# Attention with a causal bound at 64 tokens: 1280 instead of 1536 score columns per step

## The reference

```
qkv = x @ W_attn.T                       # 4 query sets, one set of keys, one of values
for g in range(4):
    att = einsum(q_g, k) / sqrt(8)       # 16 heads of 8 channels, 256 queries x 256 keys
    att = softmax(where(causal, att, -inf))
    out_g = einsum(att, v)
return concat(out_g) @ W_proj.T
```

## Time and profile before

| | us |
|---|---|
| median of 3 runs | 800.66 |
| lowest, highest | 800.66, 803.36 |
| the profiled execution | 800.58 |
| its span | 798.9 |

### The profile page before, as it was taken

How to read it: one execution, slowest core, us unless ns; L and a number is a source line. 1 busy time by engine, 2 the same in 40 slices (tenths; PEclk the granted TensorE clock), 3 DMA queues, 4 the chain that set the end, 5 groups by cost and what they waited for, 6 DMA issues and landing times.

```text
span 798.9 us, 20426 instructions
## 1 busy us (share of the span) xinstructions
PE 757.4 (95%) x7674; PEld 412.7 (52%) x7674; DVE 648.9 (81%) x1917; ACT 719.9 (90%) x932; POOL 560.2 (70%) x685
## 2 busy tenths in 40 slices
PE   5898999999999999999999999999999999999996
PEld 3345667777774333333333333333334777677774
DVE  7998999999876667777778787788566898989885
ACT  5918999999999999999999999999997999899984
POOL 2897676655437888888898888888896445444442
PEclk9999999999999999999999999999999999999999
DMA  9110000000133333442444334433500000000000
GB/s 279 61 70 29 1 2 2 2 2 1 23 94 99 98 90 89 90 99 78 96 108 106 90 88 92 90 78 96 106 2 2 1 15 16 15 14 16 15 15 18
DMA packets 37962, 45.70 MB, mean 57 GB/s; under 512 B 6137, under 2 KB 23810, under 8 KB 37858
## 3 DMA queue, kind: packets, MB, share of 16 engines
q1 hardware_dynamic: 37858, 44.33, 22.4%
HBM read 27.53 MB, written 16.78 MB: 55 GB/s over the span
## 4 chain that ended last, share of the span: by engine, by line
PE 56%; ACT 18%; DVE 12%; issue 10%; POOL 2%; DMA 0%; ACTq 0%; DVEq 0%; POOLq 0%
PE psum L1006 15%; PE psum L937 14%; ACT prob L1272 13%; PE psum L1316 12%; PE psum L1263 5%; PE psum L1374 4%; DVE mixed L1025 4%; PE psum L1154 2%; ACT hidden_first L951 2%; ACT hidden_parts_first L953 1%; PE psum L686 1%; DVE hidden_parts_first L960 1%; POOL yhat L666 1%; DVE prod L656 1%; DVE stats L362 1%
## 5 line engine op out<-in xcount | busy, mean ns | idle before, releaser
L1272 ACT ACTIVATE prob<-psum 128x1536 f32<-128x1536 f32 x256 | 347.6, 1503 | 14.5 <-PE psum L1263 14.5
L1279 POOL TENSOR_SCALAR_AFFINE_SELECT prob<-prob 128x512 f32<-128x512 f32 (+3 forms) x448 | 304.8, 709 | 42.2 <-ACT prob L1272 32.1
L1316 PE MATMUL psum<-prob,vstack 128*32 128x256 f32 (+1 forms) x2048 | 204.9, 495 | 1.6 <-DVE o_tok L1324 1.6
L937 PE MATMUL psum<-xt_parts,w_parts 128*128 128x512 f16 x768 | 186.6, 379 | 0.0
L1025 DVE SCALAR_TENSOR_TENSOR mixed<-psum,comb_y,mixed 128x128 f32<-128x128 f32 x512 | 143.1, 339 | 1.5 <-PE psum L1006 1.5
L967 POOL TENSOR_TENSOR hidden_parts_second<-hidden_second,hidden_parts_second 128x512 f16<-128x512 f32 x64 | 77.2, 1207 | 93.6 <-ACT hidden_parts_second L953 93.6
L967 POOL TENSOR_TENSOR hidden_parts_first<-hidden_first,hidden_parts_first 128x512 f16<-128x512 f32 x64 | 79.4, 1241 | 73.2 <-ACT hidden_parts_first L953 73.2
L1263 PE MATMUL psum<-qstack,kstack 32*128 32x512 f16 x768 | 99.8, 385 | 9.1 <-ACT prob L1272 7.7
L1263 PEld LDWEIGHTS psum<-qstack,kstack 32*128 32x128 f16 x768 | 24.9, 91 | 157.3 <-ACT prob L1272 138.7
L937 PEld LDWEIGHTS psum<-xt_parts,w_parts 128*128 128x128 f16 x768 | 71.0, 98 | 64.0 <-issue 1.4
L951 ACT ACTIVATE hidden_second<-psum,b 128x512 f32<-128x512 f32 x128 | 88.3, 690 | 15.6 <-PE psum L937 12.1
(11 more groups left out here) (148 smaller groups left out, 840.9 us busy)
## 6 DMA issues: line engine op xcount, KB each, us to landing
qstack<-qk_parts SPq DMA_DIRECT2D x128, 128.0 KB, 3.6
qk_parts<-parts SPq DMA_DIRECT2D x64, 192.0 KB, 3.1
kstack<-qk_parts SPq DMA_DIRECT2D x128, 32.0 KB, 3.5
stream<-u_folded SPq DMA_DIRECT2D x4, 512.0 KB, 8.0
kept_x<-stream SPq DMA_DIRECT2D x4, 512.0 KB, 2.7
out<-mixed SPq DMA_DIRECT2D x7, 256.0 KB, 2.3
w_whole<-L_ffn_W SPq DMA_DIRECT2D x1, 1024.0 KB, 8.9
taps<-c_taps SPq DMA_DIRECT2D x1, 640.0 KB, 7.1
```

What stands on the lines that cost most here:

```text
L937: last = e.matmul(bank(u % 4), m.w1[:, w_part, ex, cols], xt_parts[:, s, x_part, :], start=(n == 0), stop=(n == len(PRODUCTS) - 1))
L1272: e.activation(prob[:, n % PROBS, :], psum[:, TILE * (n % 2):TILE * (n % 2 + 1)], ACT.Exp, scale=SCALE)\
L1279: return e.affine_select(kept, kept, [[0, kept.shape[1]], [0, 2], [sign, P]], ALU.is_ge, 0.0, base=0, channel_multiplier=-sign)
L1316: last = e.matmul(to[SLOT * lane:SLOT * (lane + 1)], vstack[:, b % 2, keys, first:first + SLOT], weights_of(n - t, lane, keys, pair), star ...
```

## The change

- The causal bound is drawn at 64 tokens inside each half of 128. Of each half, its first 64 keys (`EARLY`) meet all its 128 queries, and its last 64 keys (`LATE`) only its last 64 queries. The first half's 128 keys meet the second half's queries unmasked (`ACROSS`). The two halves' EARLY scores share a bank (64 partitions each), the LATE ones half a bank. A lane then has 512 + 256 + 512 = 1280 columns, and so has a step.
- `tensor_scores`: steps 0 and 1 of a quad issue six matmuls (two halves each of two EARLY and one LATE), of 64 columns of the array each; steps 2 and 3 issue two ACROSS of 128 columns of the array and two LATE halves of 64.
- Masks: six selects a quad in place of seven: two tiles of 768 columns for the second half's rows and again for the first half's rows, and one place of 512 (the LATE blocks of two steps) twice. A place's second select waits for its first by a semaphore and comes in the queue behind the first select of the next place.
- Sums: three a quad (EARLY 512, ACROSS 512, LATE 256) in steps 1, 2 and 3. EARLY waits for the masks of both 768-column places, ACROSS for the quad's four exponentials, LATE for all masks. The slot's two places hold the halves; the values exist in three forms.
- `PROBS` is 8, and an exponential waits for all sums of the quad two back.
- Around it: three input transpositions instead of two, 15 value matmuls instead of 6, three value copies instead of one, three row transpositions instead of one, two more memsets in the first experts.

```diff
+EARLY, LATE, ACROSS = range(3)
+BLK = P // 2
+STEPS_Q = (((EARLY, 0, 0), (EARLY, 1, BANK), (LATE, 2, 2 * BANK)),
+           ((EARLY, 2, 0), (EARLY, 3, BANK), (LATE, 1, 2 * BANK)),
+           ((ACROSS, 0, 0), (ACROSS, 1, BANK), (LATE, 3, 2 * BANK)),
+           ((ACROSS, 2, 0), (ACROSS, 3, BANK), (LATE, 0, 2 * BANK)))
+COLS = 2 * BANK + SETS * BLK
+SUMS_Q = (EARLY, ACROSS, LATE)
+MASKS_Q = 3
+PROBS = 8
...
-        for h in range(HALVES):
-            last = e.transpose(bank(at_bank(b))[:, h * P:(h + 1) * P], normed[:, HALVES * b + h, :], eye[:])
+        for at, h in ((0, 1), (P, 1), (P + BLK, 0)):
+            last = e.transpose(bank(at_bank(b))[:, at:at + P], normed[:, HALVES * b + h, :], eye[:])
...
+        places = [(slice(0, P), P, ACROSS)]
+        places += [(slice(BLK * half, BLK * (half + 1)), P * half + BLK * kind, kind) for kind in (EARLY, LATE)
+                   for half in range(HALVES)]
+        for rows, first_token, kind in places:
             for i, (w_part, x_part) in enumerate(PRODUCTS):
-                last = e.matmul(bank(6)[:, h * P:(h + 1) * P], at_x[:, s, x_part, h * P:(h + 1) * P],
+                last = e.matmul(bank(6)[rows, kind * P:(kind + 1) * P],
+                                at_x[:, s, x_part, first_token:first_token + rows.stop - rows.start],
...
+        for kind, lane, col in STEPS_Q[t]:
             at = slice(SLOT * lane, SLOT * (lane + 1))
+            queries = qstack[at, s, c].rearrange("p g (h l q) -> p h l g q", h=HALVES, q=BLK)
+            if kind == ACROSS:
+                last = e.matmul(to[:, col:col + BANK], kstack[at, s, c, P:2 * P], queries[:, 0], start=True, stop=True)
+                continue
+            for half in range(HALVES):
+                rows = slice(BLK * half, BLK * (half + 1))
+                key = P * half + BLK * kind
+                if kind == EARLY:
+                    moving, place = queries[:, half], to[rows, col:col + BANK]
+                else:
+                    moving, place = queries[:, half, 1], to[rows, col:col + SETS * BLK]
+                last = e.matmul(place, kstack[at, s, c, key:key + BLK], moving, start=True, stop=True)
...
+    def gpsimd_second_half_mask(e, m):
+        q, t = divmod(m, MASKS_Q)
+        e.wait_ge(exped, 4 * q + t + 1 + t // 2)
+        gpsimd_masked(e, mask_place(m), 0).then_inc(half_masked, 1)
+    def gpsimd_first_half_mask(e, m):
+        e.wait_ge(half_masked, m + 1)
+        gpsimd_masked(e, mask_place(m), 1).then_inc(masked, 1)
     def gpsimd_mask(e, n):
+        q, t = divmod(n, 4)
+        if t != 2:
+            m = MASKS_Q * q + min(t, 2)
+            gpsimd_second_half_mask(e, m)
+            if m:
+                gpsimd_first_half_mask(e, m - 1)
...
+    def tensor_weigh(e, q, kind, last_of_quad):
+        b, c = divmod(q, QUADS)
+        if kind == EARLY:
...
+                e.wait_ge(turned, q)
+            e.wait_ge(masked, MASKS_Q * q + 2)
+        elif kind == ACROSS:
+            e.wait_ge(exped, 4 * (q + 1))
         else:
+            e.wait_ge(masked, MASKS_Q * (q + 1))
...
-            if n >= 4:
-                at = n - n % 4 - 4
-                for i in ((), (0,), (1, 2), (3,))[n % 4]:
-                    tensor_weigh(e, at + i)
+            if n >= 4 and n % 4:
+                kind = SUMS_Q[n % 4 - 1]
+                tensor_weigh(e, n // 4 - 1, kind, kind == SUMS_Q[-1])
```

More of the change, by code:

```diff
@@ L1215, in tensor_v, with v_moves @@
             e.wait_ge(attn_done, HALVES * (BATCH - 2))
-        for h in range(HALVES):
+        places = [(slice(0, P), P, ACROSS)]
+        places += [(slice(BLK * half, BLK * (half + 1)), P * half + BLK * kind, kind) for kind in (EARLY, LATE)
+                   for half in range(HALVES)]
+        for rows, first_token, kind in places:
             for i, (w_part, x_part) in enumerate(PRODUCTS):
-                last = e.matmul(bank(6)[:, h * P:(h + 1) * P], at_x[:, s, x_part, h * P:(h + 1) * P],
+                last = e.matmul(bank(6)[rows, kind * P:(kind + 1) * P],
+                                at_x[:, s, x_part, first_token:first_token + rows.stop - rows.start],
                                 wqkv_parts[:, w_part, SETS + 1, :], start=(i == 0), stop=(i == len(PRODUCTS) - 1))
         last.then_inc(v_up, 1)
[L1222 to L1226, removed]
+    def v_moves(b):
+        source = bank(6)[:, 0:3 * D].rearrange("p (k n d) -> p k n d", n=HEADS, d=HD)
+        places = vstack[:, b % 2, :, :, :, 0:HD]
+        for half in range(HALVES):
+            rows = slice(BLK * half, BLK * (half + 1))
+            yield places[rows, 0:2, :, half], source[rows, 0:2]
+        yield places[:, ACROSS, :, 0], source[:, ACROSS]
     def scalar_v_first(e):
         e.wait_ge(v_up, 1)
-        e.wait_ge(zeroed, 3)
-        e.mul(v_places(0), v_source(), 1.0 / WSCALE).then_inc(v_copied, 1)
+        e.wait_ge(zeroed, 4)
+        for place, source in v_moves(0):
+            last = e.mul(place, source, 1.0 / WSCALE)
+        last.then_inc(v_copied, 1)
     def vector_v(e, b):
@@ L1235, in vector_v @@
         if b >= 2:
-            e.wait_ge(weighed, STEPS_B * (b - 1))
-        e.tensor_scalar(v_places(b), v_source(), 1.0 / WSCALE, None, ALU.mult).then_inc(v_copied, 1)
+            e.wait_ge(weighed, SUMS_B * (b - 1))
+        for place, source in v_moves(b):
+            last = e.tensor_scalar(place, source, 1.0 / WSCALE, None, ALU.mult)
+        last.then_inc(v_copied, 1)
     def step_of(n):
@@ L1256, in tensor_scores @@
             e.wait_ge(s_stack[s], STACK * (b // 2 + 1))
-        for i, (lane, keys, pair) in enumerate(STEPS_Q[t]):
+        for kind, lane, col in STEPS_Q[t]:
             at = slice(SLOT * lane, SLOT * (lane + 1))
[L1259 to L1264, removed]
+            queries = qstack[at, s, c].rearrange("p g (h l q) -> p h l g q", h=HALVES, q=BLK)
+            if kind == ACROSS:
+                last = e.matmul(to[:, col:col + BANK], kstack[at, s, c, P:2 * P], queries[:, 0], start=True, stop=True)
+                continue
+            for half in range(HALVES):
+                rows = slice(BLK * half, BLK * (half + 1))
+                key = P * half + BLK * kind
[4 more added lines that the diff above has]
+                last = e.matmul(place, kstack[at, s, c, key:key + BLK], moving, start=True, stop=True)
         last.then_inc(scored, 1)
@@ L1295, in weights_of, with gpsimd_masked @@
[L1295 to L1313, removed]
+    def gpsimd_masked(e, kept, half):
+        sign = 1 if half else -1
+        return e.affine_select(kept, kept, [[0, n] for n in kept.shape[1:-1]] + [[sign, BLK]], ALU.is_ge, 0.0,
+                               base=BLK * half, channel_multiplier=-sign)
@@ new lines, in gpsimd_first_half_mask, with weights_of @@
+    def gpsimd_first_half_mask(e, m):
+        e.wait_ge(half_masked, m + 1)
+        gpsimd_masked(e, mask_place(m), 1).then_inc(masked, 1)
+    def gpsimd_mask(e, n):
+        q, t = divmod(n, 4)
[4 more added lines that the diff above has]
+                gpsimd_first_half_mask(e, m - 1)
+    def weights_of(q, kind, lane):
+        t, col = next((t, at) for t, held in enumerate(STEPS_Q) for of, head, at in held if (of, head) == (kind, lane))
+        return prob[:, (4 * q + t) % PROBS, col:col + (SETS * BLK if kind == LATE else BANK)]
@@ L1314, in tensor_weigh @@
         for lane in range(LANES):
-            first = SLOT * (c * LANES + lane) + 2 * HD * (1 - pair)
-            last = e.matmul(to[SLOT * lane:SLOT * (lane + 1)], vstack[:, b % 2, keys, first:first + SLOT],
-                            weights_of(n - t, lane, keys, pair), start=(t == 0), stop=(t == 3))
+            last = e.matmul(to[SLOT * lane:SLOT * (lane + 1)],
+                            vstack[:, b % 2, kind, c * LANES + lane].rearrange("p h r -> p (h r)"),
+                            weights_of(q, kind, lane), start=(kind == EARLY), stop=last_of_quad)
@@ L1338, in vector_rows @@
             e.wait_ge(projected, HALVES * b)
-        e.transpose(o_rows[:].rearrange("p a h k t -> p (a h k t)"), o_norm[:].rearrange("p a n r -> p (a n r)"))\
+        blocks = o_norm[:, 0].rearrange("p (g l n) r -> p g l (n r)", g=SETS, l=2)
+        rows = o_rows[:, 0].rearrange("p g (l t) -> p g l t", l=2)
+        for late in range(2):
+            e.transpose(rows[:, :, 1 - late], blocks[:, :, late])
+        e.transpose(o_rows[:, 1].rearrange("p g t -> p (g t)"), o_norm[:, 1].rearrange("p n r -> p (n r)"))\
          .then_inc(rows_up, 1)
@@ L1373, in tensor_project @@
         for g in range(SETS):
[L1374 removed]
+            last = e.matmul(project_bank(b)[:, h * P:(h + 1) * P], o_rows[:, 1 - h, g, :], wproj[:, g, :],
                             start=(g == 0), stop=(g == SETS - 1))
@@ L1638, in gpsimd_clear @@
         e.wait_ge(zeroed, 1)
-        ones = vstack[:, :, :, 2 * HD:].rearrange("p s h (n r) -> p s h n r", r=SLOT)
-        e.memset(ones[:, :, :, :, HD:HD + 1], 1.0).then_inc(zeroed, 1)
```

(4 more changed lines are left out.)

77 lines of the change are left out of this document (35 added, 42 removed).

## The result

The changed kernel takes 856.01 us (median of 4 runs, 852.48 to 858.25) beside 802.01 for the kernel before (median of 4 runs, 800.66 to 804.16); the ratio is 1.0667 with a 95% interval of 1.0617 to 1.0716. Slower was forecast, but 825 us, and the time lies above the range. The sign and the mechanism (EARLY waiting for a select) came as written; the size, +54 us, is more than double the +24.5 that was forecast. Its profiled execution took 857.35 us, with a span of 855.6 for 798.9.

What follows compares the result with a forecast made beforehand. ACT's exponentials were taken to bound the kernel, with PE close behind. Four stretches made a sequence 24.25 us for 22.64; +25.8 over 16 sequences, less 1.3 at the start, gave 825 us, with an 8-in-10 range of 793 to 834.

Steps and rivals of the forecast that it cites:

- What bounds the kernel: Kernel before: ACT's exponentials set 94% of a sequence, 21.3 of 22.64 us, with PE close behind at 22.1.
- The loop: From one EARLY to the next, through ACROSS, step 3's exponential and two selects: 5.56 us, 5.96 with shape prices.
- The stretch takes the larger of this and the loop.: Each EARLY-to-EARLY stretch takes the larger of PE's issue time (3.83 us plus work beside) and the loop, 5.96.
- the two stretches that I had given to TensorE's own sum: Steps 5 to 9 at 6.08 us and 13 to 1 at 6.25, where PE's time exceeds the loop's 5.96.
- my 0.95: Value matmuls on PE, steps 13 to 1: 0.71 to 1.05 us expected, 0.95 taken.
- GpSimd's power: GpSimd's power (1167 ns) stands ahead of the LATE select in one quad: up to 0.5 us more.
- The four stretches together: One sequence of attention as 5.96, 6.08, 5.96 and 6.25 us: 24.25 for 22.64, +1.61.
- The ends: First steps, before sums exist, run at ACT's new pace, six of 0.22 us less: -1.3 us.
- The price of a tile shape inside a step: PE, steps 2 and 3 of a quad: changing tile shape costs 0.20 us each, 0.40 a quad, 1.6 a sequence.
- no price inside a step: Rival: shape changes inside a step are free, loop 5.56 us, time 799 to 807, middle 804; chance 0.24.
- The faster rival: Selects come in time, PE's matmul queue alone decides: 21.0 us a sequence, 788 for half the gain, 775 all; chance 0.16.

Runs made afterwards that it cites:

- the second experiment: Changed kernel with the ACROSS scores as two tiles of 64 columns of the array in place of one of 128; 830.7 us, ratio 1.0352.
- both edits together: Changed kernel with EARLY's second first-half select ahead of the LATE select, and ACROSS scores in 64-column tiles; 791.5 us, ratio 0.9869.

## Why the prediction was wrong, point by point

The mechanism was right and its price was not. Three steps failed: the term of the loop (5.96 us, where the runs show 6.23 and once a sequence 6.41), the clock, which had no term, and the ends of attention, which had the wrong sign.

- *What bounds the kernel.* Right, and shown: with ACT relieved of a sixth and nothing else touched, the kernel gains 0.8%, not 7%.
- *The loop.* Right as a mechanism, too small as a term: 5.96 was summed, 6.23 is the plain one. The chain of the changed kernel tells what was left out: 0.06 us from the exponential's end to the select and 0.14 from the select's end to the sum. My rows held the durations; the hand-overs between engines, which in a closed loop count each time, I left at zero, except between scores and exponential, where I took start to start. The other 0.07 are 0.54 for 0.52 from the scores of step 2 to ACROSS, 0.72 for 0.70 from the scores of step 3 to their exponential, 1.24 for 1.23 for the exponential, and 1.53 for 1.51 for the two selects.
- *"The stretch takes the larger of this and the loop."* Here the rule was right, but with 6.23 the loop sets also the two stretches that I had given to TensorE's own sum. Steps 5 to 9 took 6.22 for 6.08, with TensorE's own sum close behind the loop: EARLY starts at 440.92, 0.38 us after the scores ahead of it, where 0.34 is the least. Steps 13 to 1 took 6.22 for 6.25, and that this agrees is luck: the values took 0.73 us from start to start, near the low end of 0.71 and not my 0.95, so TensorE's sum was below the loop.
- *GpSimd's power and slower selects.* The stretch with the power (steps 1 to 5) took longer than the plain loop:

```profile
428.30 3.55 POOL L1310 TENSOR_SCALAR_AFFINE_SELECT prob<-prob 128x768 f32<-128x768 f32 x4 [0.15 <-ACT prob L1301]
431.83 1.00 POOL L384 TENSOR_TENSOR rstd<-vareps,minus_half 128x4 f32<-128x4 f32 x1
432.86 2.55 POOL L1310 TENSOR_SCALAR_AFFINE_SELECT prob<-prob 128x512 f32<-128x512 f32 x3
```

  From 428.30 GpSimd is hardly idle until EARLY starts at 434.70, which is 6.41 us after the EARLY before it. I had named the power (up to 0.5) in a rival only and left it out of the forecast. A select of 768 columns averages 939 ns over 300 to 560 us (869 in the earlier trace rows). Of 164, 122 take 0.90 to 0.91 us; the 21 that lie for over a fifth of their time beside VectorE's product of `o_tok` and `rden` (L1374) take 1.10 in the mean, and 1.11 at most. That they go together stands in the trace; no run tests it.
- *The four stretches together:* 3 x 6.23 + 6.41 = 25.1, measured 25.08, forecast 24.25. The difference of 0.83 times 16 is 13 us of the 31 that were missing.
- *The clock.* It was not in the forecast at all and cost 8 to 9.5 us, by the run that fills the waits. I had written that nothing covers EARLY's wait, and did not ask what 1.3 to 2.7 us of idle time do to TensorE itself.
- *The ends.* I took 1.3 us off for the steps before the first sum. Instead the ends added: with the clock kept, the first sequence takes 26.96 us (22.23 in the kernel before), the last but one 26.35 (22.25), and from the start of the last exponential to the end it is 195.6 (193.0). In that run the change costs 45.8 us, of which 39.0 are the steady period: 6.8 for the ends, where I had -1.3. In the first sequence of the changed kernel GpSimd stands still for 1.74 us in front of its power, waiting for VectorE, and the selects that EARLY needs stand behind that power in its queue (they start at 253.01, EARLY at 254.68). With the select moved ahead the first sequence takes 22.27 us, less than the period of that run (23.15), so this part too goes with the order of the selects. The 2.6 us behind the last exponential stay open.
- *The price of a tile shape inside a step.* Right (0.20; measured 0.20 to 0.21). Without it the period falls by 1.26 us, less than the 1.6 that eight such steps make. The rival "no price inside a step" is close to what the second experiment builds; even so the time was 830.7, not 804, for the same missing terms (its mean clock was 0.982, beside 0.996 with the waits filled).
- *The faster rival.* Its condition (a loop under 5.26, a free shape) is what both edits together fulfil; it named 788 for half the gain and 775 for all of it, and 791.5 was measured, 788.9 with the inputs later.

Of the 31 missing microseconds (856.0 - 825) 13 are the loop with its hand-overs, selects and power, 8 the clock, 8 the ends (6.8 for -1.3), and 1.3 the kernel before, whose median was 802.0 beside this result and 800.7 in the forecast.

## What to carry to other kernels

Before an engine is relieved, close the loops: follow each new wait back to where it started from, one round, and sum durations and hand-overs (here 0.06 to 0.14 us each); if the round is longer than the period, it is the new period, whatever the busy shares say. In an in-order queue the place of an instruction is a dependence of its own: EARLY needed nothing of the fourth exponential; only the select that stood ahead of its own in GpSimd's queue did, and moving EARLY's select in front of that one was worth 45 us. And a gain on an engine at 94% of the period is worth what the second engine leaves, here 0.8% of 7.

## What the hardware showed that I had not expected

- Six matmuls on 32x64 tiles in three row groups, two halves in each, start within 0.02 us and take 0.34 to 0.39 us to the next group, for the 0.32 of three on 32x128. Two shapes in one step cost 0.20 to 0.21 us more, though the row group of the second shape was idle.
- After 2.64 us without a matmul in an otherwise busy stretch TensorE ran at 1.2 GHz (a sum of 1.93 us in place of 1.07); waits of 1.25 us in the steady sequences mostly passed without that (the window from 421.00 is at 1.00), with one fall in the middle of attention. Matmuls whose result is thrown away kept the clock, and made the kernel faster by 0.9 to 1.1%.
- A select of 768 columns took 0.90 to 1.11 us, and those beside one product of VectorE (L1374) took 1.10 us in the mean.
